# A 16-expert mixture routed in three parts: 87 slot tiles in place of 57, the sends of one part beside the tiles of another, a tile's expert number loaded one tile early

## What is computed

```python
x = hidden_states.reshape(-1, D)                       # 5312 x 128, layer-normed
gate_logits = x @ gate_weight.T                        # 16 experts
top_vals, top_idx = jax.lax.top_k(gate_logits, 2)
routing_w = softmax(top_vals)
mask = any(top_idx[:, :, None] == arange(16), axis=1)
h = silu(einsum('td,efd->tef', x, w1))                 # w1: 16 x 512 x 128
h_mean = einsum('tef,te->ef', h, mask) / max(counts, 1)
y_mean = einsum('ef,edf->ed', h_mean, w2)              # one row per expert
out = einsum('tk,tkd->td', routing_w, y_mean[top_idx])
```

## Time and profile before

| | us |
|---|---|
| median of 3 runs | 2394.42 (2390.42 to 2399.57) |
| the profiled execution's own time | 2394.81 |
| its span | 2393.1 |
| the first mixture in it | 316.9 to 612.4 |

### The profile page before, as it was taken

The page is one execution under the profiler, slowest core; times in us unless marked ns, Lnnn a source line. Parts: engine busy times, 40 slices in busy tenths (PEclk is TensorE's granted clock), DMA queues, the critical chain, the costliest instruction groups (busy, mean ns, idle before and its releaser), DMA issues.

```text
span 2393.1 us, 36071 instructions
## 1 busy us (share of the span) xinstructions
PE 1963.6 (82%) x9514; PEld 1083.8 (45%) x9514; DVE 1955.9 (82%) x2945; ACT 1340.7 (56%) x1979; POOL 1533.7 (64%) x1165
## 2 busy tenths in 40 slices
PE   7676651067799678766999999999999999999998
PEld 5344440045465577643444444444444444444444
DVE  5999871066456888598999999999998999999998
ACT  3000031053144233446888878888887888888887
POOL 1344307600501798334888888888887888888887
PEclk9888875599699687857999999999999999999999
DMA  4400101241100354132344345444454444444443
GB/s 100 132 18 18 79 1 47 70 74 27 49 1 0 98 163 134 58 113 77 136 136 138 138 139 201 140 141 140 139 175 165 138 138 139 142 137 145 153 145 115
DMA packets 122750, 257.21 MB, mean 107 GB/s; under 512 B 40212, under 2 KB 56244, under 8 KB 121012
## 3 DMA queue, kind: packets, MB, share of 16 engines
q1 hardware_dynamic: 119988, 250.78, 32.7%
q0 software_dynamic: 2688, 5.44, 0.7%
HBM read 219.13 MB, written 29.59 MB: 104 GB/s over the span
## 4 chain that ended last, share of the span: by engine, by line
PE 44%; DVE 7%; issue 3%; ACT 2%; DMA 1%; POOL 0%; DVEq 0%; ACTq 0%; SPq 0%; POOLq 0%
PE bank L2015 24%; PE bank L2029 20%; DVE hc L1947 3%; ACT bank L1867 2%; DMA m_share<-expert_shares 1%; DVE hc L1951 1%; DVE bank L1944 1%; DVE m_work L1929 1%; PE bank L2036 0%; DVE m_best L1926 0%; DVE h L1955 0%; DVE m_work L1920 0%; DVE m_ut L638 0%; DVE m_best L1919 0%; DVE m_row L1912 0%
## 5 line engine op out<-in xcount | busy, mean ns | idle before, releaser
L1867 ACT ACTIVATE bank<-bank,m_b 128x896 f32<-128x896 f32 x768 | 753.0, 981 | 201.7 <-PE bank L2015 201.7
L1824 POOL TENSOR_TENSOR hc<-hc 128x896 f16<-128x896 f32 x384 | 725.3, 1889 | 32.0
L2029 PE MATMUL bank<-hc,weights 128*128 128x448 f16 x3072 | 706.9, 353 | 8.3 <-DVE h L1955 7.1
L1822 POOL TENSOR_SCALAR hc<-hc 128x896 f16<-128x896 f32 x384 | 360.8, 939 | 171.3 <-PE bank L2029 114.7
L1947 DVE TENSOR_TENSOR hc<-bank,m_share 128x896 f32<-128x896 f32 x384 | 419.0, 1091 | 52.9 <-ACT bank L1867 14.7
L2015 PE MATMUL bank<-m_u_first,weights 128*128 (+1 forms) x1536 | 421.9, 356 | 28.7 <-DVE hc L1947 12.3
L2029 PEld LDWEIGHTS bank<-hc,weights 128*128 128x128 f16 x3072 | 298.7, 98 | 297.1 <-issue 15.4
L1944 DVE TENSOR_TENSOR bank<-bank,m_share 128x896 f32<-128x896 f32 x384 | 418.5, 1090 | 10.9 <-ACT bank L1867 6.2
L1951 DVE TENSOR_TENSOR hc<-bank,hc 128x896 f16<-128x896 f32 x384 | 415.1, 1081 | 5.4 <-ACT hc L1870 5.4
L2015 PE MATMUL bank<-m_u_second,weights 128*128 (+1 forms) x1536 | 417.6, 354 | 0.0
L1870 ACT ACTIVATE hc<-bank 128x896 f16<-128x896 f32 x384 | 351.7, 916 | 38.4 <-DVE bank L1944 25.9
(11 more groups left out here) (300 smaller groups left out, 2562.5 us busy)
## 6 DMA issues: line engine op xcount, KB each, us to landing
m_share<-expert_shares SPq DMA_DIRECT2D x384, 448.0 KB, 3.6
ew_raw<-e_w_dram SPq DMA_DIRECT2D x32, 512.0 KB, 4.5
expert_factors<-ew_made SPq DMA_DIRECT2D x24, 512.0 KB, 3.1
weights<-expert_factors SPq DMA_DIRECT2D x12, 1024.0 KB, 9.5
expert_slots<-lru_zeros SPq DMA_DIRECT2D x1, 7296.0 KB, 28.2
lru_wst<-w_dram SPq DMA_DIRECT2D x16, 256.0 KB, 2.7
weights<-w_dram SPq DMA_DIRECT2D x1, 4096.0 KB, 12.4
xs<-x_dram SPq DMA_DIRECT2D x4, 996.0 KB, 12.7
```

Source lines behind the costliest of these rows:

```text
L1822: g.tensor_scalar(h_first[:, x, 1], hs[:, x], 1.0 - SHARE, 1.0, ALU.mult, ALU.mult).then_inc(first_of[1], 1)
L1824: g.tensor_tensor(h_second[:, x, 1], hs[:, x], h_first[:, x, 1], ALU.subtract).then_inc(second_of[1], 1)
L1867: sc.activation(bank, bank, ACT.Gelu, bias=b1[:, bass.ds(grp * GE + e, 1), c]).then_inc(gelu[c], 1)
L2029: last = t.matmul(banks_y[:, q], k.weights[:, grp % 2, 2 + m, at], hh[:, e % 2, c, q * HW:(q + 1) * HW], start=(grp > 0 and e == 0 and c = ...
```

## The change

The 42 tiles of tokens are cut into `PARTS` = 3 parts of 14. Each part has its own range of `NSP` = 29 slot tiles, and each expert its own whole tiles within every part. So there are 87 slot tiles in place of 57, and `k.slots` has 22272 rows in place of 14592.

- VectorE forms the tokens of one part, then routes that part (`route(p)`), then goes on with the next. Each of its arrays is a third as wide. TensorE and ScalarE interleave in the same way: TensorE does one part's token products, then waits for that part's mask, then its two ranking products.
- GpSimd sends a part's 28 indirect DMAs as soon as that part's slots are there. SP loads a part's tiles when that part's sends have landed: 10 loads to a part (the last with two tiles), 30 in all.
- TensorE turns the routing weights (42 transposes, four to a group, eleven groups) inside the loop over tiles, after every fifth tile, and ScalarE copies them there, after that tile's silu.
- The expert number of tile j+1 is read after the fourth of tile j's eight matmuls.
- The counts of the parts are added behind the routing, and `owned`, `picked` are 16 x 87.

```diff
+PARTS = 3
+NSP = (2 * (NTW // PARTS) * TW + E0 * (ST - 1)) // ST
+NST = PARTS * NSP
...
-            sp.wait_ge(sent, 16 * 2 * NTW)
-            for g in range(NL):
+            for g in range(PARTS * LPP):
+                if g % LPP == 0:
+                    sp.wait_ge(sent[g // LPP], 16 * 2 * TPP)
                 if g >= RING:
-                    sp.wait_ge(up, PER * (g - RING + 1))
-                sp.dma_start_transpose(xt[:, g % RING], k.slots[g * PER * ST:(g + 1) * PER * ST, :]).then_inc(x_in[g % RING], 16)
+                    sp.wait_ge(up, last_tile(g - RING) + 1)
+                start, end = (g // LPP * NSP + g % LPP * PER) * ST, (last_tile(g) + 1) * ST
+                sp.dma_start_transpose(xt[:, g % RING, :, 0:end - start], k.slots[start:end, :]).then_inc(x_in[g % RING], 16)
...
             pool.wait_ge(k.zeroed, 16)
-            pool.wait_ge(second, NCW)
-            pool.wait_ge(slots, 1)
             for n in range(NTW):
+                if n % TPP == 0:
+                    pool.wait_ge(slots, n // TPP + 1)
...
+            for p in range(PARTS):
+                for b in banks_of(p):
+                    tokens(b)
+                dve.wait_ge(second, banks_of(p)[-1] + 1)
+                route(p)
...
+            def turn(x):
+                c, n = turns[x]
+                if x == 0:
+                    pe.wait_ge(shared, PARTS)
+                if x >= 2:
+                    pe.wait_ge(rt_ready, x - 1)
+                for q in range(n):
+                    last = t.transpose(turn_bank(x)[:, q * TW:(q + 1) * TW], wt[:, c + q], k.ident[:])
                 last.then_inc(turned, 1)
-            pe.wait_ge(rt_ready, NCW)
-            pe.wait_ge(owners, 1)
+            def expert_of(j):
+                if j < NST:
+                    if j % NSP == 0:
+                        pe.wait_ge(owners, j // NSP + 1)
+                    return pe.value_load(owner_i[0:1, j:j + 1], min_val=0, max_val=E0 - 1)
+
+            pe.wait_ge(second, NCW)
             pe.wait_ge(k.w0_split, NC)
+            following = expert_of(0)
             for j in range(NST):
-                g, r = j // PER, j % PER
+                g, r = load_of(j)
+                expert = following
                 if r == 0:
                     pe.wait_ge(x_in[g % RING], 16 * (g // RING + 1))
                 if j >= SETS:
                     pe.wait_ge(summed, j - SETS + 1)
-                expert = pe.value_load(owner_i[0:1, j:j + 1], min_val=0, max_val=E0 - 1)
                 for f in range(FC):
                     bank = set_banks(j)[:, f // 2, f % 2 * ST:(f % 2 + 1) * ST]
                     for m in range(2):
                         last = t.matmul(bank, w0_parts[m][:, bass.ds(expert * FF0 + f * 128, 128)],
                                         xt[:, g % RING, m, r * ST:(r + 1) * ST], start=(m == 0), stop=(m == 1))
+                    if f == 1:
+                        following = expert_of(j + 1)
                 last.then_inc(up, 1)
+                if j % 5 == 4 and j // 5 < len(turns):
+                    turn(j // 5)
```

More of the change, by code:

```diff
@@ L708, in first_mixture @@
         rt_ready = sem("rt_ready")
[L709 removed]
+        sent = [sem(f"rows_sent{p}") for p in range(PARTS)]
         x_in = [sem(f"x_in{p}") for p in range(RING)]
@@ L775, in _ @@
             act.wait_ge(scaled, 1)
[L776 to L786, removed]
+            for p in range(PARTS):
+                for b in banks_of(p):
+                    act.wait_ge(product, b + 1)
+                    for q in range(3):
+                        n = 3 * b + q
+                        last = sc.activation(u_tok[:, n, 0], token_banks(b)[:, q, 0:128], ACT.Identity, scale=scale[:, n:n + 1])
+                    last.then_inc(first, 1)
+                act.wait_ge(centred, p + 1)
+                sc.activation(gap[:], gap[:], ACT.Exp).then_inc(expd, 1)
             load_table(nc, k, 1, ACT.Silu)
@@ L815, in _ @@
                 last.then_inc(second, 1)
[L816 to L825, removed]
@@ L836, in _ @@
[L836 to L840, removed]
-            count, whole, ends, start = few[:, 0], few[:, 1], few[:, 2], few[:, 3]
-            v.tensor_tensor(halves(place[:]), halves(upto[:]), totals, ALU.subtract)
@@ L889, in _ @@
             pe.wait_ge(gate_in, 17)
-            for b in range(NCW):
-                if b >= 4:
-                    pe.wait_ge(second, b - 3)
-                for q in range(3):
-                    m = 3 * b + q
-                    last = t.matmul(token_banks(b)[:, q], k.hc[:, m * TW:(m + 1) * TW], gi[:], start=True, stop=True)
-                last.then_inc(product, 1)
-            pe.wait_ge(counted, 1)
-            pe.wait_ge(made, 8)
-            for q in range(2):
-                t.matmul(k.bank[:, 4 + q, 0:HALF_E * NTW], before[:], halves(mask[:])[:, q], start=True, stop=True)
-                last = t.matmul(k.bank[:, 6 + q, 0:HALF_E * NTW], every[:], halves(mask[:])[:, q], start=True, stop=True)
@@ L902, in _ @@
-            last.then_inc(ranked, 1)
-            pe.wait_ge(shared, 1)
-            for c in range(NCW):
-                if c >= 4:
-                    pe.wait_ge(rt_ready, c - 3)
-                for q in range(3):
-                    last = t.transpose(k.bank[0:E0, c % 4, q * TW:(q + 1) * TW], wt[:, 3 * c + q], k.ident[:])
-                last.then_inc(turned, 1)
-            pe.wait_ge(rt_ready, NCW)
-            pe.wait_ge(owners, 1)
+            for p in range(PARTS):
+                for b in banks_of(p):
+                    if b >= 4:
+                        pe.wait_ge(second, b - 3)
+                    for q in range(3):
+                        m = 3 * b + q
+                        last = t.matmul(token_banks(b)[:, q], k.hc[:, m * TW:(m + 1) * TW], gi[:], start=True, stop=True)
+                    last.then_inc(product, 1)
+                pe.wait_ge(masked, p + 1)
+                pe.wait_ge(made, 8)
+                if p:
+                    pe.wait_ge(slots, p)
+                t.matmul(within, before[:], flat(mask), start=True, stop=True)
+                t.matmul(totals, every[:], flat(mask), start=True, stop=True).then_inc(ranked, 1)
```

158 lines of the change are left out of this document (102 added, 56 removed).

## The result

The changed kernel takes 2436.49 us (2430.28 to 2440.72, 4 runs), the kernel before on the same chip 2393.35: a ratio of 1.0175 [1.0144, 1.0205]. The forecast was 2377, within 2358 to 2400. The profiled execution took 2440.72, 63.6 us over the forecast. Times within a kernel (starts, gaps, stretches) are read from its one profiled execution.

A forecast was written before the change was run, and what follows sets the result against it. POOL's send rate was taken to bound the sends, TensorE's sequencer the tile loop (1.7 us a tile). Terms: -93.0 + 51.8 + 7 + 3 + 13.5 = -17.7 from 2394.8, giving 2377 us, range 2358 to 2400.

The forecast's parts named there:

- the start of the tile loop: Loop's first matmul, after part 1's routing and 28 sends: at 382.5 in place of 475.5, 93.0 us earlier.
- POOL goes on without a pause: Sends of parts 2 and 3: landed at 413 and 449, not binding, 20 and 35 us of room.
- The 158: Tile loop: 158 us from the first tile's first matmul to the last tile's.
- the odd tile: Near the start of the kernel before's tile loop: one tile 2.9 us over a normal period.
- Rival (c): Part 1's sends beside routing: VectorE holds them up; priced at 25 us, 2402; chance 0.12.
- Sends and first load: From the mixture's start: first send after 22 us, the 28th 36 us later.
- Tiles: Tile loop: 30 more tiles at 1.725 us each, +51.8 us.
- turning inside the loop: Tile loop: 42 weight transposes now in TensorE's order, +7 us, bounds 4 and 9.
- Early number: Tile loop: reading the expert number in the middle of the tile before gains 0; upper bound +9 us.
- Rival (a): Tile loop: the expert number's reading is hidden and VectorE paces; 38 us less, 2339; chance 0.12.
- Zeroing: Recurrence: the larger slot-zeroing DMA lands after 43.0 us, not 28.2, and delays the chain: +13.5 us.
- Gather: After the tile loop: 16 x 87 array in place of 16 x 57, VectorE paces the rounds, +3 us.

The follow-up runs named there:

- y2: Kernel after, but GpSimd waits ahead of send 29 for all three parts' slots, with no wait ahead of send 57: 2368.16 us, one run.
- y1: Kernel after with the token work of all three parts ahead of the first part's routing: 2374.47 us, ratio 0.9919.
- experiment 1: Kernel after with all sends held until all parts are routed: 2404.33 us; with all loads behind all sends too: 2470.95 us.
- experiment 8: Kernel before with early expert number: ratio 0.9996; with zeroing queued last: 0.9986; kernel after with zeroing queued last: 1.0112, 2422.90 us.
- z1: Kernel after, but GpSimd's waits ahead of sends 29 and 57 both ask for all three parts' slots: 2439.15 us, ratio 1.0183.
- experiment 9: Kernel after with two parts in place of three, all sends behind all routing, zeroing queued last: 2370.07 us, ratio 0.9893.

## Why the prediction was wrong

**The step that failed is the start of the tile loop**, and with it "POOL goes on without a pause". I let VectorE end the third routing near 372 (55 us from the mixture's start, on its clock), beside sends that would at worst slow themselves. In the kernel after it ends at 442.0, 110 us from the start. The loop's first matmul comes 106.2 us after the mixture's start (437.8 - 331.6) in place of 66: 40 us. The second stretch of sends starves the loop as well: from its first matmul to the last tile's it took some 181 us in place of 158, 23 more (some 7 of them because VectorE was still busy with the late routing at the fourth tile). 40 + 23 = 63, all of the miss. The 158 held 7 us for turning and the odd tile's 2.9, neither of which comes in a clean loop (148 us in y2); against that loop the starving cost 33 us, and two forecast terms that failed hide ten of them.

**The right risk, the wrong victim.** Rival (c) had VectorE hold up the sends. For 10 us VectorE was 96% busy and the sends took their usual 0.96; it was VectorE, ScalarE and TensorE's sequencer that stood. The Trainium skill ("SBUF — State Buffer", "SBUF: two separate sides") has GpSimd blocked from writing descriptors while VectorE runs an operation in a mode that takes the shared ports too; the prediction read it as holding beside VectorE at large. No row tells which of VectorE's operations here, if any, ran in such a mode, and in the sends' median nothing of it shows. On a small scale something like it is there: of the 84 sends four took over 1.05 us, and each of them overlaps an operation of VectorE on two arrays in SBUF (TENSOR_TENSOR). The longest is this one, which began beside one such operation and went on beside the next:

```profile
446.28 1.45 POOL L800 DMA_INDIRECT expert_slots<-m_u_tok,m_slot  x1 [0.30 <-issue]
...
446.93 1.61 DVE L917 TENSOR_TENSOR m_owned<-m_owned,m_counts 128x1392 f32<-128x1392 f32 x1
```

In all that is 1.2 us over the kernel's sends. The traces of all 19 kernels with indexed sends agree: no send over 1.05 us without such an operation beside it, the longest of all 2.04 us. In the kernel before, the first two sends (1.21 and 1.42) ran beside one, and the third, which took 0.96, began ahead of its own. The prediction took the low value from that third send, and for the size of (c) that was right.

**The mechanism forecast is real where nothing is starved.** y2: first matmul at 395.5, 64.7 us after the mixture's start (66 predicted), 2368.16 us in all. y1: 2374.5. The gain forecast exists, and the kernel after, on its chip, doesn't get it.

The other terms:
- *Sends and first load*: first send 22.6 us after the start (22 predicted), SP's first load 36.8 after that (36.2 and landing). Right.
- *Tiles*: 87 at 1.72 us (1.725) in y2 and experiment 1. Right. These loops have the turning in them at this pace, and 57 tiles without it take 1.71 (the early number alone), so **turning inside the loop** costs 1 us or so over 86 periods and not 7: mis-sized. The prediction's own terms give 5.3 (4.2 and eleven waits of 0.1); it took 7.
- *Early number*: 0, right. Rival (a) falls: it would have given 25 us in the 57 tiles of experiment 8. How deep TensorE's queue is, no run here shows; only the gain that the prediction drew from it didn't come.
- *Zeroing*: landing after 42.1 us (43.0 predicted), mixture 14.7 later, of which 1.3 was there at the recurrence's start: 13.4 (13.5 predicted). Right. This is the row of the zeroing in the kernel after:

```profile
L456 SPq DMA_DIRECT2D expert_slots<-lru_zeros x1: 654/654/654, 55.7 to 55.7; - x1
...
DMA to landing us min/median/max: 42.1/42.1/42.1
```

- *Gather*: from the loop's end to the mean row's copy (ym) 20.7 us in place of 18.6, 2.1 for 3:

```profile
622.22 2.63 DVE L924 TENSOR_TENSOR m_picked<-m_owned,m_part 128x1392 f32<-128x1392 f32 x1
...
642.89 0.28 DVE L927 COPY m_ym<-bank 16x128 f32<-16x128 f32 x1 [3.76 <-PE bank L993]
```

**What stays open.** Which step failed is shown; what puts an execution into this state is not. It is there from the second send, so before anything in y2's and the kernel after's work differs; kinds of work, restarts, content and number of waits have been tried. z1 excludes that the slots asked for ahead of the 29th send save it; the rest was tried only on chips where nothing was starved, or came out starved where everything with indexed sends did, and is open. It stays through the runs of one build on one chip: all four timed runs of each starved kernel are slow, all four of y1 and of experiment 9 fast. Whether the build or the chip decides, or both, isn't shown; y2's clean time is a single run. That lost records and late instructions have one cause is argued from their going together, not shown. Nor is it shown that an execution without the profiler's records would be starved, since every run here was recorded. y2 with the late zeroing, 2368 - 14 by the terms above, wasn't tried.

## What to carry to other kernels

Work moved beside a stretch that was idle isn't free because the engines are: ask whether the trace shows anything strange there now. Here it was one tile of 2.9 us and landings without a time. When a change of order loses time in a way that the sum can't hold, first run the same kernel again on another chip, and then vary its code on one chip, with the kernel itself among the variants. Here variants were clean or starved by 71 us, 3%, and because each set ran on its own chip, eighteen of them can't say whether code or chip decided. And a large transfer ahead of a queue's loads can cost what it delays (13.4 us here; queued last, the kernel after was 13.6 us shorter).

## What the runs showed of the hardware

Beside indexed sends from GpSimd (one each 1.27 us) the instructions of VectorE, ScalarE and TensorE's sequencer can come late. In the kernel after they were late by 0.7, 1.4 and up to 16.5 us, from 10 us into the sends until 4 to 7 us behind them, with the sends' own median of 0.962 us untouched; in z1 one tile followed another only after 22.4 us. In the one build with plain sends (0.54 us each) this didn't appear, nor in the clean builds with indexed ones. Two kernels that differ in one wait, long met when it is reached (y2 and z1), differ by 71 us, on two chips. Where this happened, 238 to 277 of the sends' 1344 records of landing were left. An indexed send that runs beside a VectorE operation on two arrays in SBUF can take longer: in the ten kernels whose operations on arrays of 128x1392 ran beside sends, two sends took 1.34 to 2.04 us and the one ahead of them kept 0.96. In 19 traces no send took over 1.05 us without such an operation beside it.
